# Splitting the softmax reciprocal over VectorE, ScalarE and GpSimd in a fused attention and mixture-of-experts kernel

## What is computed

```python
q = rope((layernorm(x) @ Wq)); k = rope(ctx @ Wk); v = ctx @ Wv
w = softmax(q @ k.T / sqrt(16))           # per head
x = x + (w @ v) @ Wout + bout
x = x + shared_ffn(layernorm(x)) + sum_over_two_best_experts(layernorm(x))
```

## Time and profile before

| what | value |
| --- | --- |
| median of three runs | 665.83 us |
| profiled execution | 665.54 us, of which the span of its instructions is 663.8 us |
| granted clock of PE, mean | 0.987 of full speed |
| PE busy | 603.5 us, 91% of the span |
| DVE busy | 489.9 us, 74% |
| ACT busy | 369.7 us, 56% |
| POOL busy | 383.5 us, 58% |
| chain that ended last | PE 72%, DVE 8%, DMA 7% |

### The profile page before, as it was taken

The page is one execution under the profiler, slowest core; times in us unless marked ns, Lnnn a source line. Parts: engine busy times, 40 slices in busy tenths (PEclk is TensorE's granted clock), DMA queues, the critical chain, the costliest instruction groups (busy, mean ns, idle before and its releaser), DMA issues.

```text
span 663.8 us, 17290 instructions
## 1 busy us (share of the span) xinstructions
PE 603.5 (91%) x6016; PEld 365.0 (55%) x6016; DVE 489.9 (74%) x914; ACT 369.7 (56%) x620; POOL 383.5 (58%) x454
## 2 busy tenths in 40 slices
PE   2757999999999999689999999999999799999991
PEld 0234555555555555356666566666666466666660
DVE  7687899999999998754759746676677366766771
ACT  4256566666766676673311136666576366666660
POOL 3766687778888886322000024487646687776761
PEclk9989999999999999999999999999999899999996
DMA  8456687666445556512425623855897745446842
GB/s 307 88 129 151 154 145 168 144 124 130 121 121 121 130 134 163 130 55 92 144 80 186 235 80 111 257 133 116 262 253 208 197 91 95 75 83 177 243 79 35
DMA packets 108978, 95.37 MB, mean 144 GB/s; under 512 B 72640, under 2 KB 77248, under 8 KB 108928
## 3 DMA queue, kind: packets, MB, share of 16 engines
q1 hardware_dynamic: 97184, 68.15, 38.2%
q0 software_dynamic: 8752, 20.71, 16.1%
q10 hardware_dynamic: 2992, 5.85, 2.8%
HBM read 70.12 MB, written 23.07 MB: 140 GB/s over the span
## 4 chain that ended last, share of the span: by engine, by line
PE 72%; DVE 8%; DMA 7%; issue 4%; POOL 3%; SPq 2%; ACT 2%; POOLq 0%; DVEq 0%; ACTq 0%
PE p_sc L754 14%; PE p_sc L723 13%; PE p_qk L723 12%; PE p_qk L538 8%; PE p_v L538 7%; DMA used_twice_too<-used_twice 4%; PE p_pv L625 3%; PE p_tr L717 3%; PE p_sc L586 2%; PE p_pv L741 2%; PE p_sc L607 2%; SPq L429 2%; DVE negmax L1141 2%; PE p_sc L610 2%; DMA xe<-xn_dram,from_at 1%
## 5 line engine op out<-in xcount | busy, mean ns | idle before, releaser
L1141 DVE TENSOR_REDUCE negmax<-p_sc 128x4 f16<-128x512 f32 x128 | 80.7, 680 | 11.2 <-PE p_sc L586 11.0
L849 ACT ACTIVATE prob<-p_sc 128x512 f32<-128x512 f32 x128 | 69.9, 606 | 25.9 <-PE p_sc L610 18.0
L984 ACT CAST hiddenT<-p_pv 128x384 f16<-128x384 f32 x54 | 25.9, 479 | 99.5 <-PE p_pv L741 99.5
L1550 POOL COPY from_at<-from_rows 128x1 uint32 (+1 forms) x40 | 32.9, 824 | 80.6 <-DVE from_rows L1392 77.3
L1570 POOL DMA_INDIRECT out<-prob,to_at x38 | 69.1, 1818 | 12.2 <-issue 11.8
L754 PE MATMUL p_sc<-used_twice,hiddenT 128*128 128x512 f16 (+1 forms) x306 | 71.6, 379 | 0.0
L723 PE MATMUL p_qk<-used_twice,xeT 128*128 128x352 f16 x420 | 68.4, 313 | 0.6 <-DMA xeT<-xn2T_dram 0.6
L723 PE MATMUL p_sc<-used_twice,xeT 128*128 128x352 f16 x420 | 68.4, 312 | 0.0
L1272 DVE TENSOR_TENSOR hidden<-p_sc,act_g 128x352 f32<-128x352 f32 x55 | 28.8, 523 | 51.7 <-PE p_sc L723 29.5
L963 ACT COPY xeT<-p_tr 128x1024 f16<-128x1024 f16 x40 | 40.5, 1012 | 38.3 <-PE p_tr L717 38.3
L1289 DVE TENSOR_SCALAR prob<-p_sc,gate_at 128x512 f32<-128x512 f32 x38 | 28.5, 751 | 39.0 <-PE p_sc L754 37.7
(11 more groups left out here) (181 smaller groups left out, 1436.2 us busy)
## 6 DMA issues: line engine op xcount, KB each, us to landing
w<-e SPq DMA_DIRECT2D x20, 1408.0 KB
w<-e SPq DMA_DIRECT2D x20, 512.0 KB
out<-stream SPq DMA_DIRECT2D x17, 256.0 KB, 2.4
values<-weighed SPq DMA_DIRECT2D x32, 128.0 KB, 2.0
xn_dram<-xn_parts SPq DMA_DIRECT2D x16, 256.0 KB, 2.0
xn2T_dram<-xn2T SPq DMA_DIRECT2D x16, 256.0 KB, 2.2
w<-e SPq DMA_DIRECT2D x20, 192.0 KB
xeT<-xn2T_dram SPq DMA_DIRECT2D x14, 256.0 KB, 2.9
```

The lines of the kernel that those rows point to most:

```text
L849: act.activation(prob[:, c % RING, :], p_scored(c)[:], ACT.Exp, scale=SCALE).then_inc(exp_ready, 1)
L1141: dve.tensor_reduce(negmax[:, c % 2, at:at + CH], p_scored(c)[:].rearrange("p (h t) -> p h t", t=P), AX_X, ALU.max, negate=True).then_inc( ...
L1550: pool.tensor_copy(from_at[:, par, u:u + 1], from_rows[:, bass.ds(q, 1)]).then_inc(from_copied, 1)
```

## The change

The sums are loaded twice, into rows 0 to 31 and 32 to 63. DVE inverts all 64 rows in one instruction and does no more. ACT rounds the 64 rows to float16 (`recip_high`). POOL subtracts in place in rows 32 to 63 (`recip_low`). PE's `spread_recip` waits for POOL instead of DVE. DVE's next reciprocal, SP's next load and ACT's next copy wait on new semaphores.

```diff
-        sums = sb("sums", [HEADS, P])
-        recip = sb("recip", [HEADS, P])
+        sums = sb("sums", [2 * HEADS, P])
+        recip = sb("recip", [2 * HEADS, P])
@@ load_sums (SP)
-                    sp.wait_ge(recip_step, b * 3 - 2)
-                sp.dma_start(sums[:], sums_dram).then_inc(sums_loaded, 16)
+                    sp.wait_ge(recip_made, b)
+                for part in range(2):
+                    sp.dma_start(sums[part * HEADS:(part + 1) * HEADS], sums_dram).then_inc(sums_loaded, 16)
@@ spread_recip (PE)
-                pe.wait_ge(recip_step, b * 3 + 3)
+                pe.wait_ge(recip_lo, b + 1)
@@ scalar
+            def recip_high(b, par):
+                act.wait_ge(recip_made, b + 1)
+                if later(b, 1):
+                    act.wait_ge(spread_done, b)
+                act.copy(recip16[:], recip[:]).then_inc(recip_hi, 1)
...
                 on(-1, q_high)
+                on(-3, recip_high)
@@ vector
             def sums_invert(b, par):
-                dve.wait_ge(sums_loaded, b * 16 + 16)
-                dve.reciprocal(recip[:], sums[:]).then_inc(recip_step, 1)
-                dve.wait_ge(recip_step, b * 3 + 1)
...
-                dve.tensor_tensor(recip16[0:HEADS], recip[:], ones16[0:HEADS, :], ALU.mult).then_inc(recip_step, 1)
-                dve.wait_ge(recip_step, b * 3 + 2)
-                dve.tensor_tensor(recip16[HEADS:2 * HEADS], recip[:], recip16[0:HEADS], ALU.subtract).then_inc(recip_step, 1)
+                dve.wait_ge(sums_loaded, b * 32 + 32)
+                if later(b, 1):
+                    dve.wait_ge(recip_lo, b)
+                dve.reciprocal(recip[:], sums[:]).then_inc(recip_made, 1)
@@ gpsimd
+            def recip_low(b, par):
+                pool.wait_ge(q_parts, min(b + 3, B) if isinstance(b, int) else b + 3)
+                if isinstance(b, int) and b + 3 > B:
+                    pool.wait_ge(xn2_lo, b - 1)
+                pool.wait_ge(recip_hi, b + 1)
+                pool.tensor_tensor(recip16[HEADS:2 * HEADS], recip[HEADS:2 * HEADS], recip16[HEADS:2 * HEADS], ALU.subtract).then_inc(recip_lo, 1)
+                pool.wait_ge(recip_lo, b + 1)
...
                 on(-2, q_low)
+                on(-4, recip_low)
                 on(-1, k_sum)
```

More of the change, by code:

```diff
@@ L254, in build @@
         shifted = sem("shifted"); exp_ready = sem("exp_ready")
-        pv_done = sem("pv_done"); weighed_kept = sem("weighed_kept"); recip_step = sem("recip_step")
+        pv_done = sem("pv_done"); weighed_kept = sem("weighed_kept"); recip_made = sem("recip_made"); recip_hi = sem("recip_hi"); recip_lo = sem("recip_lo")
         values_moved = sem("values_moved"); sums_stored = sem("sums_stored"); sums_loaded = sem("sums_loaded")
@@ L434, in store_sums @@
                 if later(b, 1):
-                    sp.wait_ge(sums_loaded, b * 16)
+                    sp.wait_ge(sums_loaded, b * 32)
                     sp.nop().then_inc(turning, 1)
@@ L1150, in sums_invert @@
             def sums_invert(b, par):
-                dve.wait_ge(sums_loaded, b * 16 + 16)
-                dve.reciprocal(recip[:], sums[:]).then_inc(recip_step, 1)
-                dve.wait_ge(recip_step, b * 3 + 1)
+                dve.wait_ge(sums_loaded, b * 32 + 32)
                 if later(b, 1):
-                    dve.wait_ge(spread_done, b)
-                if not later(b, 1):
-                    dve.wait_ge(consts, 1)
-                dve.tensor_tensor(recip16[0:HEADS], recip[:], ones16[0:HEADS, :], ALU.mult).then_inc(recip_step, 1)
-                dve.wait_ge(recip_step, b * 3 + 2)
-                dve.tensor_tensor(recip16[HEADS:2 * HEADS], recip[:], recip16[0:HEADS], ALU.subtract).then_inc(recip_step, 1)
+                    dve.wait_ge(recip_lo, b)
+                dve.reciprocal(recip[:], sums[:]).then_inc(recip_made, 1)
             def normalise(b, par):
```

## The result

| kernel | runs | median us | ratio to before, 95% interval |
| --- | --- | --- | --- |
| before, first three | 3 | 665.83 | |
| changed, first series | 6 | 676.0 (666.74 to 677.13) | 1.0153 [1.0089, 1.0218] |
| changed, second series | 4 | 676.8 (673.08 to 678.06), before there 666.32 | 1.0219 [1.0083, 1.0355] |

The change makes the kernel slower by about 10 us. The first six runs lie in two groups, two at 666.7 and 667.6 and four from 675.4 to 677.1. Forecast were 669.3 and a range of 665.7 to 673.0: the sign was right, the size not.

What follows compares the result with a forecast made beforehand. Attention was taken to be bound by PE. Spread 0.85, ACT's queue 0.6, loads 1.25 and tail 0.8 made 3.5 us on 665.54, so 669.0, and 669.3 with the runs' median 0.29 higher; range 665.7 to 673.

Steps and rivals of the forecast that it cites:

- The loads: Batches 1, 3 and 4: loads issued later, beside SP's transposes, cost 1.25 us in one of three rounds.
- The spread: PE's `spread_recip` starts later behind `q_low`, after POOL's subtraction: 0.85 us over ten rounds, bounds -0.4 and +3.2.
- the faster rival: DVE free 1.7 us earlier each round, later work moves up: at most 3.0 us gained, 662.8; chance 0.08.
- one of my own signs of being wrong: In the loop: the forecast is wrong if the stretch of the loop gets shorter.
- ACT's queue at batch 1: Load issues behind the waiting copy start the exponentials 0.97 later; less 0.37 slack, PE loses 0.6, bounds 0 and 1.8.
- The tail: Batches 14 and 15: exponentials 0.49 later, DVE's pieces after the weight split 0.3 later; about 0.8, bounds 0.3 and 1.3.
- SP's extra load: One more small load per batch on SP, issue priced at 0.35 us, delaying values and a store; counted as 0.
- The much slower rival: Loads and transposes collide in every round with a load, or POOL's subtraction takes 0.67 or more: about 673; chance 0.13.

Runs made afterwards that it cites:

- n6: Changed kernel with weight loads early and the load of x late, scatter of routed results left out: 659.94 us.
- n3: Changed kernel with all loads ahead of ACT's copy, scatter of routed results left out: 655.67 us.
- e1: Changed kernel with ACT's load issues of steps 3 to 7 put ahead of its copy: 665.23 us, ratio 0.9993 to before.
- r2: Changed kernel unaltered, a third time, one run: 673.76 us.
- n5: Changed kernel with the load of x early and weight loads late, scatter of routed results left out: 655.53 us.
- n1: Kernel before with the scatter of routed results left out: 653.04 us.
- e6: Kernel before with ACT's load issues of steps 2 to 7 moved ahead of `k_high`: 665.78 us, ratio 1.0026 to before.
- e8: Kernel before with ACT's load issues of steps 3 to 7 alone moved ahead of `k_high`: 665.55 us, ratio 1.0024 to before.
- e2: Changed kernel with only step 3's load of x put ahead of ACT's copy: 666.03 us, ratio 1.0020 to before.
- e3: Kernel before, with ACT's queue made to wait for DVE's reciprocal ahead of its load issues in steps 3 to 7: 670.27 us, ratio 1.0078.
- r1: Changed kernel unaltered, timed again beside the kernel before: 676.8 us, ratio 1.0219.
- n2: Changed kernel with the scatter of routed results left out: 660.97 us.
- e5: Changed kernel with step 3's load of x cut from five rows to two, the rest loaded in step 2: 670.22 us, ratio 1.0121 to before.
- e4: Changed kernel with loads ahead of ACT's copy and the copy at the very end of a step: 664.81 us, ratio 1.0011 to before.

## Why the prediction was wrong, point by point

**The loads (1.25, bounds 0 to 3.75): the step that failed.** The mechanism was right, a load that the copy makes late collides with transposes; the size was wrong: 5.1 to 7.1 in the traces from batch 0 to 15, 4.3 to 5.8 in the times without gathers. I priced only the weight loads of steps 4 to 7 and forgot that step 3's load of x stands behind the same copy. The weight loads, on which I spent the term, cost 0 to 1.0; the load of x cost 4.3 (n6 - n3). Its price stood in the trace of before, in step 2, where the same load is issued shortly ahead of the same kind of transposes; timeline of ACT's and SP's queues, kernel before:

```profile
39.44 0.38 ACTq L952 DMA_DIRECT2D stream<-x  x1
...
40.10 6.23 SPq L429 DMA_TRANSPOSE used_twice_too<-used_twice  x2
```

6.23 against 4.01 in batch 0's round is 2.2 us more of PE's wait, and this row would have put the sum near 671.5. The fall of PE's clock behind a longer wait I had in no term. With 5.3 in place of 1.25 the sum is 7.6, close to the 7.9 without gathers; that is partly luck, since the spread and ACT's queue were priced too high and something that I have not traced makes up for it.

**The rule that speaks for it.** SP's pairs got longer in the rounds with two late weight loads: at batch 1, 3.29 instead of 2.64, at batch 2, 4.69 instead of 3.90, at batch 3, 3.57 instead of 2.71; at batch 4, with one load, 2.70 instead of 2.65. That agrees with the Trainium skill (DMA: Bandwidth & Descriptors, "Queues, rings and completion order"), by which each DMA engine takes turns between the queues that have work; no run here shows the packets. I had used it only to ask how many of three rounds would pay. PE's waits for transposes in the rounds of batches 1 to 4 were 0.17 to 0.93, where they were 0.55 to 0.91 without the change, so the slowing came in three rounds and little of the cost.

**The spread (0.85).** The durations came as worked out (0.42 for 0.43, 0.64 for 0.57 to 0.62), the sum did not: rounds of the loop became 0.06 us shorter, not 0.05 to 0.10 longer. I had kept `q_low`'s start fixed against the reciprocal, and it moved ahead by 0.17. What pulls it was not tried. I had held against the faster rival that nothing in `q_low`'s chain gets shorter; that was wrong too, though it is worth only 0.2 us over the four rounds measured. A shorter loop was one of my own signs of being wrong.

**ACT's queue at batch 1 (0.6).** The exponentials start 0.98 us behind the reciprocal's end, where I had 1.02:

```profile
81.57 0.30 ACT L869 CAST recip<-recip 64x128 f16<-64x128 f32 x1 [1.33 <-DVE recip L1162]
81.57 0.35 ACTq L954 DMA_DIRECT2D w<-s  x1
81.95 0.45 ACTq L957 DMA_DIRECT2D w<-s  x1
82.51 1.58 ACT L850 ACTIVATE prob<-p_sc 128x512 f32<-128x512 f32 x3 [0.64 <-PE p_sc L611]
```

PE's group that needs the fourth starts at 85.12, right behind the value projection (84.20 and 0.82): cost 0.1, the slack was larger. The row of the exponentials names PE as what they waited for, but PE had been done by 81.98; the second issue ended at 82.40.

**The tail (0.8).** The copy starts at 288.72 and the exponentials 0.2 behind it. From batch 14 to 15 it takes 14.48 us instead of 13.30, but 13.63 in e1, r2 and n5, and 13.85 in n1 with the old reciprocal: about 0.3 by the instructions (13.63 and 13.30 are both at full clock), the rest by PE's clock, which in the changed kernel is granted at 0.53 in the stretch behind the wait for the spread:

```profile
289.75:291.75 2.00, 2.00 (x36) 1.64 (x35) 1.56 (x3) 1.78 (x4) 0.08 (x1) 0.53 0.00 0
```

With the 0.5 us behind the mark (n3 against n1) the term of 0.8 was about right. The clock fell there in some traces with the old reciprocal too (n1, e6, e8), so what the fall costs is not put down to the change.

**The rest.** SP's extra load was counted as 0; no run tests it by itself. DVE's reciprocal of 64 rows took 0.94 and its lines 1158 and 1160 went, 24.5 us of busy time less (489.9 to 465.4), for nothing, as forecast. The much slower rival (about 673), at a chance of 0.13, had the right mechanism and came nearest, but put the collisions into the wrong rounds. The wait for a gather (4.5 us) was visible in the trace of before; traces with and without such a wait differ by 3 to 7 us behind the mark, and the forecast and its range took no account of it.

## What to carry to other kernels

When an instruction that waits is put into an engine's program, list every DMA issue behind it, in each written-out step, with its size, and look in the trace for the same transfer issued at the new distance: here its time to landing, less the distance, told how long the transfer behind it took. Count the load that is late by its victim: here 1280 KB just ahead of transposes cost 4 us, while four steps of smaller loads cost next to nothing, and the cure was to issue the loads ahead of the wait, as they had been. When a trace holds one rare wait of several us, compare two kernels at a mark ahead of it, or leave out the work that causes it in both.

## What the runs showed of the hardware

- Two DMA transposes took 2.64 us issued 3.45 us behind a load of 1280 KB on another queue (e2), 4.01 at 2.2 behind it (before), 4.69 at 1.75 (r2), and 6.00 to 6.25 at 0.6 (changed, e3, r1, n2); behind 512 KB at 0.6 they took 2.92 (e5). The slowed pairs ended 0.1 to 0.4 us ahead of the load's landing.
- Behind a store of 2 x 8 KB issued 0.7 us after such a load, the reload of the sums came 3.0 us later than without it (e8 against before).
- PE's clock fell to 0.66 to 0.75 in the stretches behind waits of 2.31 to 4.39 us (n5, n6, changed, e3) and stayed whole behind 1.87, 1.95 and 2.13 (before, e1, n3): in batch 0's round of the changed kernel 2.45 us more of waiting went with 1.3 us more by the clock. It fell without such a wait too, to 0.57 from 58 to 62 us in r2 and e2.
- A POOL subtraction of 32x128 took 0.42 us, and 0.93 beside DVE's pieces of 128x512 (e4).
